# State-space stage: TensorE's chunk-state products behind the x projection, VectorE's state steps and remainder ahead of the convolution taps

## The reference, cut to what matters

```python
proj = hidden_states @ in_proj_w.T                       # 2 sequences x 512 tokens, width 512
gate, xBC, dt = jnp.split(proj, [INTER, INTER + CONV_DIM], axis=-1)   # INTER = 8192
conv = causal depthwise convolution of xBC with 4 taps, + conv_b
x, Bm, Cm = jnp.split(silu(conv), ...)                   # 8 groups, state size 128
# chunks of 128 tokens, 128 heads of 64:
scores = jnp.einsum('bclhn,bcshn->bchls', Cc, Bc) * Lmat
Ydiag  = jnp.einsum('bchls,bcshp->bclhp', scores, xdt)
states = jnp.einsum('bclhn,bchl,bclhp->bchpn', Bc, decay_states, xdt)
new    = carry * chunk_decay + states                    # from chunk to chunk
Yoff   = jnp.einsum('bclhn,bchpn,bchl->bclhp', Cc, prev, jnp.exp(cs))
y = Ydiag + Yoff + x * D
yg = y * silu(gate)
out = (grouped rms norm of yg) * norm_w @ out_proj_w.T
```

## Time and profile before

| | |
|---|---|
| runs, us | 2484.07, 2487.39, 2491.2 (median 2487.39) |
| span of the profiled execution | 2482.8 us |
| what the median has beyond that span | 4.6 us |
| TensorE busy | 2378.8 us, 96% |
| VectorE busy | 1787.9 us, 72% |
| ScalarE busy | 1591.7 us, 64% |
| GpSimd busy | 1232.0 us, 50% |
| mean granted TensorE clock | 0.986 |

### The profile page before, as it was taken

One profiled execution on the slowest core, in us unless ns is written; L12 is line 12 of the kernel. 1 busy time (PEld: TensorE's weight loads), 2 busy tenths in 40 slices (PEclk: granted clock), 3 DMA queues, 4 the chain that ended last, 5 costly groups with the idle time before them and its releaser, 6 DMA issues. The chain is left out here.

```text
span 2482.8 us, 48888 instructions
## 1 busy us (share of the span) xinstructions
PE 2378.8 (96%) x15424; PEld 1368.9 (55%) x15624; DVE 1787.9 (72%) x3234; ACT 1591.7 (64%) x3327; POOL 1232.0 (50%) x986
## 2 busy tenths in 40 slices
PE   6999999999999999999999998879999999999797
PEld 3555555555555555555555555445555555555443
DVE  6777777777777777777777776577777777788522
ACT  7676776776776776776776775265665656656422
POOL 4455555555555556556556459344434343454223
PEclk8999999999999999999999999999999999999999
DMA  7343343343343343343343341230110110100000
GB/s 248 108 129 111 108 128 111 108 133 105 113 132 107 110 133 109 106 137 109 102 140 109 119 151 56 103 124 1 43 43 1 44 44 1 43 18 1 1 0 34
DMA packets 113827, 218.79 MB, mean 88 GB/s; under 512 B 9632, under 2 KB 43040, under 8 KB 111360
## 3 DMA queue, kind: packets, MB, share of 16 engines
q1 hardware_dynamic: 113536, 215.28, 26.6%
HBM read 212.10 MB, written 3.15 MB: 87 GB/s over the span
## 5 line engine op out<-in xcount | busy, mean ns | idle before, releaser
L256 DVE SCALAR_TENSOR_TENSOR xc<-bank,taps,xc 128x511 f32<-128x511 f32 (+2 forms) x384 | 284.7, 742 | 44.6 <-ACT xc L243 27.4
L984 ACT ACTIVATE E<-wq,cst 128x128 f32<-128x128 f32 x1024 | 311.8, 390 | 2.2 <-PEq L298 2.2
L1268 POOL TENSOR_TENSOR xw<-xt,wdec 128x384 f32<-128x384 f32 x128 | 106.4, 832 | 327.3 <-DVE xt L1119 163.7
L1277 POOL TENSOR_TENSOR acc<-acc,sq 128x512 f32<-128x512 f32 x112 | 172.0, 1536 | 186.8 <-ACT sq L996 186.8
L1911 POOL TENSOR_TENSOR qT<-qT,qrot 128x512 f32<-128x512 f32 x64 | 81.3, 1270 | 368.6 <-DVE qrot L1801 368.6
L1161 DVE SCALAR_TENSOR_TENSOR u<-xc,D,bank 128x512 f32<-128x512 f32 x128 | 95.6, 747 | 210.3 <-PE bank L813 198.8
L1100 DVE TENSOR_TENSOR E<-E,cbm 128x1024 f32<-128x1024 f32 x128 | 242.9, 1898 | 0.8
L61 PE MATMUL bank<-xhi,wx 128*128 128x512 f16 x640 | 242.5, 379 | 0.0
L60 PE MATMUL bank<-xlo,wx 128*128 128x512 f16 x640 | 242.5, 379 | 0.0
L59 PE MATMUL bank<-xhi,wx 128*128 128x512 f16 x640 | 242.5, 379 | 0.0
L1263 POOL TENSOR_TENSOR ecs<-ecs,xcC 128x768 f32<-128x768 f32 x128 | 234.1, 1829 | 0.4 <-POOLq L298 0.4
(11 more groups left out here) (237 smaller groups left out, 6299.4 us busy)
## 6 DMA issues: line engine op xcount, KB each, us to landing
wq<-cs_rows SPq DMA_DIRECT2D x128, 512.0 KB, 4.1
ecs<-ecs_rows SPq DMA_DIRECT2D x128, 384.0 KB, 3.6
wx<-in_w_xbc SPq DMA_DIRECT2D x80, 256.0 KB, 2.7
wz<-in_w_z SPq DMA_DIRECT2D x64, 256.0 KB, 2.7
wo<-in_w_o SPq DMA_DIRECT2D x64, 256.0 KB, 4.0
wq<-in_wq SPq DMA_DIRECT2D x8, 1024.0 KB, 5.7
awo<-in_wo SPq DMA_DIRECT2D x8, 1024.0 KB, 5.0
wkv<-in_wkv SPq DMA_DIRECT2D x8, 512.0 KB, 3.7
```

The source lines that it names most:

```text
L256: self.nc.vector.scalar_tensor_tensor(out=dst[:, d:T], in0=self.k.bank[bank][:, 0:T - d], scalar=self.taps[:, bass.ds(g, 1), b, j, 3 - d:4 ...
L984: ins = nc.scalar.activation(E[t.i % 4][:, h, c], sc.csr[t.i % 2][:, h, c * P:(c + 1) * P], ACT.Relu, scale=-1.0, bias=head(sc.cst, t, c, h))
L1277: nc.gpsimd.tensor_tensor(acc[t.b][:], acc[t.b][:], sq[:], ALU.add).then_inc(acc_done, 1)
```

## The change

On TensorE `states(n1)` stands behind the x projection instead of ahead of it, in all slots that have a tile three ahead (0 to 124). On VectorE the state steps and the remainder stand together behind `masked` and ahead of the taps: step 0, remainder, steps 1 and 2, taps. In the last three slots the order is as before. GpSimd's `accumulate` gets one more wait on its own semaphore, in the first slot of each unit.

```diff
                     s = tile_at(g, m)
                     scan(s)
-                    if tile_at(g, m + 1):
-                        states(tile_at(g, m + 1))
+                    t, n1 = tile_at(g, m + 3), tile_at(g, m + 1)
+                    if n1 and not t:
+                        states(n1)
                     if s.i == 0 and not (isinstance(s.u, int) and s.u == 0):
                         pe.wait_ge(bt_done, s.u + 1)
                         sum_squares(1 - s.b, s.u, s.n)
-                    t = tile_at(g, m + 3)
                     if t:
                         free_bank(s)
                         pe.wait_ge(sc.wx_ok, t.g * CT + (t.i + 3))
                         sc.project(sc.wx[2 + t.i], t.b, ring_bank(s.b, x_use(s)), sc.xp_ready)
+                        states(n1)
...
-                    if n1:
+                    if n1 and not n3:
                         state(n1, 0)
                     dve.wait_ge(y_done, s.n + 1)
                     nc.vector.tensor_tensor(u[s.i % 2][:], u[s.i % 2][:], gz[s.i % 2][:], ALU.mult).then_inc(yg_done, 1)
-                    if n1:
+                    if n1 and not n3:
                         state(n1, 1)
                         state(n1, 2)
+                    if n1:
                         masked(n1)
...
-                            if d < 3 and behind[d - 1]:
-                                behind[d - 1]()
...
                     if n3:
-                        taps("x", sc.xc[n3.i % 4], n3, 2 + n3.i, (remainder, None))
+                        state(n1, 0)
+                        remainder()
+                        state(n1, 1)
+                        state(n1, 2)
+                        taps("x", sc.xc[n3.i % 4], n3, 2 + n3.i)
...
                 def accumulate(t):
                     if t.i == 0:
+                        wait(pool, acc_done, t.n)
                         pool.sem_inc(acc_done, 1)
                         return
```

More of the change, by code:

```diff
@@ L1172, in slot, with taps @@
                         mean_square(s.u, s.b)
-                    def taps(kind, dst, t, j, behind=(None, None)):
+                    def taps(kind, dst, t, j):
                         q = conv_of_slot(s, kind)
```

## The result

The changed kernel takes 2513.86 us (median of 4 runs, 2511.05 to 2515.09) against 2486.03 us (4 runs): a ratio of 1.0105, 95% interval 1.0093 to 1.0117, so it is slower by about 28 us. The forecast was 2507 us, slower by 20; the time lies in the range, and the direction was right. Its terms were not: the one behind the jumps was twice too large, the ones for wolo and for the last unit were far too small, and TensorE's own, put at nothing, was a gain of 10 us.

What follows compares the result with a forecast made beforehand. TensorE, busy 96% of the span, was taken as the bound. Added waits of 11 + 8 + 1 = 20 us on 2482.8 gave 2502.8, plus 4.6 from span to median 2507.4 us; range 2489 to 2530.

Steps and rivals of the forecast that it cites:

- TensorE is the bound and has no wait to lose: Changed stage: TensorE, busy 96% of the span, sets its time; a reordering can gain only through TensorE's boundaries.
- TensorE's order costs nothing: TensorE, x ahead of line 821: same instructions and boundary costs, sum 0; bounds per slot 0.2 us gained to 0.1 lost.
- I take the boundary step as unchanged: TensorE, scan into x: costs the same step as scan into line 821, so x starts at about 1102.22 in slot 89.
- An ordinary slot loses nothing, by 0.04 us: Slot 89: state steps end in time for line 830's load, 1107.92 against a limit of 1107.96; no loss.
- The second rival: Ordinary slots late too: about 95 slots lose 0.15 to 0.3 us each, about 2528 us; chance 0.24.
- (a): Slots behind a jump back, where `u` starts late: state steps 1.6 us late in seven slots, 11 us.
- (b): Eight units with wolo, which may start just ahead of masked: two slots each at 0.5 us on average, 8 us.
- (c): Last unit, where GpSimd is full: four slots at 0.3 us, 1 us, since TensorE later waits for GpSimd anyhow.
- The third rival: TensorE takes x behind the scan without the boundary step: 0.2 us gained in 125 slots, 2482 us; chance 0.06.

Runs made afterwards that it cites:

- experiment 5: Kernel before, with state steps behind masked and the remainder between the taps on VectorE, TensorE's order as before: 2487.83 us, ratio 1.0006.
- experiment 1: Changed kernel with VectorE's remainder put back behind the first tap, so the three state steps follow each other: 2476.07 us, ratio to before 0.9957.
- experiment 4: Changed kernel with VectorE's order of before, so only TensorE's part of the change: 2578.0 us in one run.
- experiment 7: As experiment 1, with the sum of squares of a finished unit also behind the x projection: 2476.1 us, ratio to before 0.9955.
- experiment 8: As experiment 7, with the sum of squares behind the chunk-state products instead of ahead of them: 2474.43 us, ratio to before 0.9949.
- experiment 3: Changed kernel with GpSimd's wolo behind acc instead of ahead of it: 2490.08 us, ratio to before 1.0006.

## Why the prediction was right or wrong, step by step

*TensorE is the bound and has no wait to lose: right.* The kernel before and experiment 5 have the same TensorE list and another VectorE order, and their ordinary slots are equal within 2 ns.

*TensorE's order costs nothing: wrong by 10 us.* The step named was "I take the boundary step as unchanged". Its working added the 0.11 us of a weight load, so x was to start 0.42 us behind the merged row's start (1102.22 against 1101.80); it started 0.32 us behind it (1050.13 against 1049.81), no later than line 821 had. Scan-to-x costs 0.09 us less than scan-to-products in each ordinary slot (experiments 1 and 5). The stated bounds, 0.2 less to 0.1 more, held it; the middle was the wrong choice. What I called equal, because the array's width changes in the same way, depends on what comes first behind it. The rule of the Trainium skill's TensorEngine Tiling (Array Packing), Key Properties, that a change of mode drains the engine, agrees with the trace as far as the step itself goes: x, too, starts its first matmul 0.32 us behind the start of the last merged row. That the engine drains there no run shows.

*An ordinary slot loses nothing, by 0.04 us: right, with 0.3 us of room in slots 90 to 95 (5.7 against 6.0).* A dependent neighbour follows `u` after 0.78 us and not 0.89, and acc, started earlier, is sooner gone. In the second units nothing is waited outside slot 9, and 0.06 us there. The second rival, in which ordinary slots are late too, didn't come.

The Trainium skill, SBUF — State Buffer, the section on the physical sides of the memory, has whichever of VectorE with two inputs in that memory and GpSimd starts first hold the shared port for its whole instruction. Taken as strictly as the prediction took it, that the other then needs its own whole length, it didn't come out: the remainder ended 0.55 us behind acc in slots 82, 83 and 89, as in the earlier trace rows, and not 0.74. The order of start fits in slots 82 and 89. In slot 83 the remainder's record starts 0.01 us ahead of acc's, both while wolo still ran (to 1053.86), and it was the remainder that was held; no run varies which of two that wait for a third comes first.

*(a) Behind a jump back 11 us: more than twice too large.* Slots 1 waited 4.9 us in all. Of these 0.6 belong to slot 1 itself, whose `u` came on time and which wolo made late; the six slots behind a jump waited 0.3 to 0.9 us each and not 1.6, slot 113 0.15. In those six the wait was `u`'s start, counted from the start of the scan's last matmul, less 0.72 us. `u` as late as in slot 81 before (1.77 us) would thus have cost 1.05 us and not 1.3. The 0.35 us by which VectorE's list is longer did not push `u`: it started after 1.04 to 1.63 us (1.13 in slot 81), before after 1.37 to 2.55, and only in slot 97 later than before. Why it came earlier stays open.

*(b) wolo 8 us: far too small, and the step that failed.* I worked slot 83 out at 0.8 us and then took two such slots a unit at 0.5, without a reason for the count. There were four in every unit, slots 2 to 5, and in half of the units slot 7 too, for 22.3 us in all; slot 83 itself had 0.70. I had thought of wolo only as something that delays masked when it starts just ahead of it. In slot 83 it started behind masked and did as much harm, since it moved acc behind itself and the remainder behind acc. In these slots masked mostly starts 1.8 us behind the scan's last matmul and wolo anywhere from 1.1 to 2.7; acc comes behind both, and either order ends with the remainder held by acc.

*(c) The last unit 1 us: 5.8.* GpSimd has an instruction at nearly every moment there, and the remainder took 2.10 us in slot 122. The forecast had it cheap because TensorE waits for GpSimd later anyhow; the stage's last two slots were 1.0 us shorter than before, so at most that was given back.

*The sum.* 11 + 8 + 1 + 0 = 20 was forecast; 4.9 + 22.3 + 0.4 + 5.8 - 10 = 23.4 was found (0.4 is slot 9), 1.4 more in the stage, and 3.8 us outside it that no edit explains. That the total was near is luck: the errors had both signs, with wolo and the last unit 19 us too small, the jumps 6 too large and TensorE's own 10 us left out. The 4.6 us by which the median before lay above the profiled span were 2.5 for the changed kernel, which brought the forecast of the time 2 us nearer than that of the span (2502.8 against 2511.4). The third rival, faster by the boundary, was true in part: 10 of the 25 us that it named are real, hidden under the waits, and without them experiment 1 shows them.

## What to carry to other kernels

An instruction that nobody on the critical path needs must not stand between a producer and the engine that waits for it, above all if it can be held by another engine: count for every instruction of such a chain whom it can queue behind, and not only how long it takes alone. When one engine is at its floor, the boundaries between its kinds of work are what a reordering can win, here 0.09 us each. And the parts of a change should be timed apart: here TensorE's order was worth -10 us (experiment 1 against 5), the place of the remainder +38 (changed kernel against 1), and TensorE's order with VectorE's old one +90 (experiment 4).

## What the runs showed of the hardware that was not expected

- Behind products on half the array's width, a 512-column bf16/fp16 matmul has its successor after 0.227 us (0.216 elsewhere), while an fp32 128-column product has its successor after 0.214 us (0.111 elsewhere): 0.09 us per boundary, in 110 slots 10 us (experiments 1 and 5).
- Behind one-column fp32 products the first step of the next fp32 products is 193 ns instead of 109 (experiments 7 and 8), which costs 0.08 us. In experiment 7 each one-column product and the first product behind them start 0.03 us behind their own weight loads, which follow one another at 0.11 us, while the later products start 0.11 us behind theirs. I take it that such short products can't hide a load; no run measured that by itself.
- The first step inside line 830's fp32 transposes is 0.166 us instead of 0.109 when they had to wait: 2.9 us over the 55 slots with a wait (changed kernel).
- Swapping two GpSimd instructions changed a VectorE instruction's duration from 1.82 to 0.83 us (slot 83, experiment 3).
